# Routing of a two-block kernel spread over its steps, weights by tanh, and an expert part without loops on two engines

## What is computed

```python
mu, cov = mean and grouped covariance of x over all tokens        # groups of 16 channels
wm  = five Newton steps for the inverse root of cov
x   = gamma0 * (wm @ (x - mu)) + beta0
t   = layernorm(x)
a   = softmax(t . t[window of 33 tokens] / 8) @ t[window]         # same tokens are queries, keys, values
y   = x + layernorm(a) * gamma1 + beta1
n   = layernorm(y)
probs  = softmax(n @ router.T)                                    # 8 experts
rw, re = top_k(probs, 2);  rw = rw / sum(rw)
out = y + n + sum over the chosen e of rw[e] * (gelu(n @ w1[e] + b1[e]) @ w2[e] + b2[e])
```

## Time and profile before

| | |
|---|---|
| median of three timed runs | 1159.38 us |
| lowest and highest | 1153.58 and 1163.94 us |
| the profiled execution | 1151.54 us, its span 1149.7 us |
| mean granted TensorE clock in it | 0.942 of full |
| instructions | 27099 |
| busy: PE, DVE, ACT, POOL | 1070.4, 912.9, 570.3, 148.5 us |
| second part, first L968 to the end of step 55 | 78.6 to about 539 us |
| expert part | about 578 to 1149 us |

### The profile page before, as it was taken

One profiled execution on the slowest core, in us unless ns is written; L12 is line 12 of the kernel. 1 busy time (PEld: TensorE's weight loads), 2 busy tenths in 40 slices (PEclk: granted clock), 3 DMA queues, 4 the chain that ended last, 5 costly groups with the idle time before them and its releaser, 6 DMA issues.

```text
span 1149.7 us, 27099 instructions
## 1 busy us (share of the span) xinstructions
PE 1070.4 (93%) x9158; PEld 707.9 (62%) x9158; DVE 912.9 (79%) x2575; ACT 570.3 (50%) x919; POOL 148.5 (13%) x179
## 2 busy tenths in 40 slices
PE   7957999999999999998699999999999999999998
PEld 7835777777777777777554555555555555555553
DVE  6943578968898989898888787777787877778785
ACT  0013455545555555554355555555555555555553
POOL 7021222212222222222100000000000000000000
PEclk9956699959999999998599999999999999999999
DMA  9504355544545555555112222222222222222221
GB/s 291 219 8 92 87 140 129 129 101 117 139 121 141 128 131 136 129 135 121 54 49 64 71 68 68 70 66 72 65 71 68 68 72 64 71 71 65 71 68 45
DMA packets 244738, 111.41 MB, mean 97 GB/s; under 512 B 199392, under 2 KB 242656, under 8 KB 243888
## 3 DMA queue, kind: packets, MB, share of 16 engines
q1 hardware_dynamic: 235456, 96.91, 33.7%
q10 hardware_dynamic: 8064, 12.85, 3.3%
q0 software_dynamic: 1136, 0.56, 0.2%
HBM read 71.60 MB, written 38.67 MB: 96 GB/s over the span
## 4 chain that ended last, share of the span: by engine, by line
PE 69%; DVE 17%; ACT 6%; issue 3%; DMA 2%; SPq 1%; POOL 0%; DVEq 0%; ACTq 0%; POOLq 0%
PE p L1127 16%; PE p L1102 15%; PE p L1112 9%; PE p L1076 5%; PE p L960 5%; PE p L1049 4%; PE p L953 3%; PE p L970 3%; ACT prob L558 3%; DVE arena L646 2%; DVE t_s L816 2%; PE p L1071 2%; ACT xt_s L506 2%; DMA resid<-in_x_dram 2%; PE p L1123 2%
## 5 line engine op out<-in xcount | busy, mean ns | idle before, releaser
L575 ACT ACTIVATE arena<-p,b_s 128x896 f32<-128x896 f32 x224 | 225.4, 1007 | 245.9 <-PE p L1102 245.2
L869 DVE TENSOR_TENSOR arena<-arena,p 128x896 f32<-128x896 f32 x224 | 242.8, 1084 | 91.7 <-PE p L1112 88.3
L1127 PE MATMUL p<-arena,w_s 128*64 128x448 f32 x896 | 215.3, 559 | 0.3 <-DVE arena L869 0.3
L1102 PE MATMUL p<-thl,w_hi 128*128 128x448 f32 x448 | 164.8, 449 | 0.5 <-DVE thl L843 0.5
L1102 PE MATMUL p<-thl,w_lo 128*128 128x448 f32 x448 | 127.6, 366 | 0.0
L1112 PE MATMUL p<-arena,selector 128*128 128x448 bf16 x448 | 123.8, 358 | 3.6 <-DVE arena L869 3.2
L1112 PEld LDWEIGHTS p<-arena,selector 128*128 128x128 bf16 x448 | 25.4, 97 | 160.9 <-issue 115.6
L1102 PEld LDWEIGHTS p<-thl,w_hi 128*128 128x128 f32 x448 | 85.6, 192 | 21.1 <-issue 0.6
L464 POOL TENSOR_TENSOR yb<-yb,bet 128x448 f32<-128x448 f32 x56 | 59.3, 1059 | 275.3 <-DVE xn_s L810 275.3
L1076 PEld LDWEIGHTS p<-arena 64*96 64x96 f32 x1568 | 78.4, 175 | 21.6 <-issue 21.6
L766 DVE TENSOR_REDUCE sm<-sq 128x14 f32<-128x896 f32 (+1 forms) x59 | 61.2, 1037 | 38.3 <-ACT sq L530 32.5
(11 more groups left out here) (176 smaller groups left out, 1675.8 us busy)
## 6 DMA issues: line engine op xcount, KB each, us to landing
tn_spill<-tnt_s ACTq DMA_DIRECT2D x56, 224.0 KB, 2.4
arena<-tn_spill SPq DMA_DIRECT2D x56, 224.0 KB, 3.3
t_s<-tn_spill SPq DMA_DIRECT2D x56, 224.0 KB, 2.5
arena<-in_x_dram SPq DMA_DIRECT2D x112, 96.0 KB, 2.3
xn_rows<-xn_s SPq DMA_DIRECT2D x56, 192.0 KB, 2.1
out_dram<-arena SPq DMA_DIRECT2D x112, 96.0 KB, 1.8
resid<-in_x_dram SPq DMA_DIRECT2D x6, 1568.0 KB, 15.4
v_a<-xn_rows SPq DMA_DIRECT2D x56, 168.0 KB, 3.3
```

The costliest lines, as they stand in the source:

```text
L575: a.activation(hid[:, j % 2, :].rearrange("p (h n) -> p h n", h=H), (p34 if j % 2 == 0 else p56)[:, :, 0:CH], ACT.Gelu, bias=b1_s[:, j:j + ...
L869: v.tensor_tensor(gated[:, j % 2, :].rearrange("p (h n) -> p h n", h=H), hid[:, j % 2, :].rearrange("p (h n) -> p h n", h=H), p01[:, :, 0: ...
L1102: last = t.matmul(bank[:, h, 0:CH], w[:, 128 * j:128 * (j + 1)], thl[:, c, h, :], start=(k == 0), stop=(k == 1))
L1127: last = t.matmul(p2[64 * h:64 * h + 64, 0:CH], w2_s[:, j, :], gated[:, j % 2, h * CH:(h + 1) * CH], start=False, stop=(j == 3))
```

## The change

- SyncE: the token loads of group g+3 are issued ahead of the rows of group g instead of behind them.
- Routing: 19 operations a pair (the copy is k = -1), one a step from step 13 on, in the slot ahead of the wait for the reciprocal root; in the seven drain steps two a step, the second in the slot behind t_s; then two a group in the expert part, behind gate 0 and gate 2, until all eight pairs are done in group 47. By the end of the drain three pairs are routed.
- The tile `logits` is gone. ScalarE copies the logits straight into `comb`, where the weights of the same tokens will be written later; k = -1 copies them from there.
- Weights: the first two pairs keep the exponential. From the third on ScalarE computes h = tanh(gap / 2), and the weights are 0.5 - 0.5 h and 0.5 + 0.5 h, three instructions without a reciprocal.
- Expert part: VectorE and ScalarE are written out group by group; TensorE and SyncE keep their loops.
- Before the first group of each pair VectorE waits for that pair's weights.

```diff
-        logits = sb("logits", [128, NB * CPI, E])
+ROUTE_STEPS = 19
+ROUTE_FROM = 13
...
+        def route_turn(g, slot):
+            if g < G:
+                return g - ROUTE_FROM if slot == 0 else -1
+            if g < G + 7:
+                return G - ROUTE_FROM + 2 * (g - G) + slot
+            return G - ROUTE_FROM + 14 + 2 * (g - G - 7) + slot
+        def route_at(g, slot):
+            n = route_turn(g, slot)
+            return (n // ROUTE_STEPS, n % ROUTE_STEPS - 1) if 0 <= n < NP * ROUTE_STEPS else (NP, None)
+        LATE = 2
...
             for g in range(G + 1):
+                if g + 3 < G:
+                    tokens_in2(g + 3)
                 if g < G:
                     rows_out(g)
-                if g + 3 < G:
-                    tokens_in2(g + 3)
                 if g > 0:
                     values_in(g - 1)
...
-                    a.activation(logits[:, cq * NB:(cq + 1) * NB, :], p2[:, CH:CH + NB * E].rearrange("p (b e) -> p b e", b=NB),
+                    to = comb[:, q * NB * EM:(q + 1) * NB * EM].rearrange("p (b e) -> p b e", e=EM)[:, :, 0:E]
+                    a.activation(to, p2[:, CH:CH + NB * E].rearrange("p (b e) -> p b e", b=NB),
                                  ACT.Copy).then_inc(s_ls, 1)
...
+            def share(g, slot):
+                im, k = route_at(g, slot)
+                if k == 11:
+                    assert im >= LATE
+                    wait(act, s_gap, im + 1)
+                    a.activation(top[:, 3, :], top[:, 2, :], ACT.Tanh, scale=0.5).then_inc(s_gexp, 1)
...
             def step3(g, c, has, i, first=0):
                 if has(0):
                     for j in range(first, 2):
                         gelu(g, c, j)
+                    share(G + 7 + g, 0)
...
                     gelu(g, c, 2)
                     gelu(g, c, 3)
+                    share(G + 7 + g, 1)
...
-            step3(1, 1, lambda d: d <= 1, 0)
-            step3(2, 0, lambda d: True, 1)
-            act.wait_ge(s_gap, NP)
-            a.activation(top[:, 3, :], top[:, 2, :], ACT.Exp).then_inc(s_gexp, 1)
-            step3(3, 1, lambda d: True, 1)
-            with act.Fori(2, G // 2 - 1) as i:
-                step3(i * 2, 0, lambda d: True, i)
-                step3(i * 2 + 1, 1, lambda d: True, i)
...
+            for g in range(1, G + 1):
+                step3(g, g % 2, lambda d, g=g: d <= g < G + d, g // 2)
...
+                if k < 0:
+                    dve.wait_ge(s_ls, CPI * (im + 1))
+                    v.tensor_copy(pick[:, 2], weights_of(im)).then_inc(s_top, 1)
+                    return
...
+                if k == 12 and im >= LATE:
+                    ins = v.tensor_scalar(top[:, 0, :], top[:, 3, :], 0.5, None, ALU.mult)
+                if k == 13 and im >= LATE:
+                    ins = v.tensor_scalar(top[:, 1, :], top[:, 0, :], -1.0, 0.5, ALU.mult, ALU.add)
+                if k == 14 and im >= LATE:
+                    ins = v.tensor_scalar(top[:, 2, :], top[:, 0, :], 0.5, None, ALU.add)
...
-                routed = None if im is None or c == 5 else 3 * ((c + 1) % 7)
-                if routed is not None:
-                    route(im, routed)
-                    route(im, routed + 1)
+                im, k = route_at(g, 0)
+                if im < NP:
+                    route(im, k)
...
-                if routed is not None:
-                    route(im, routed + 2)
+                im, k = route_at(g, 1)
+                if im < NP:
+                    route(im, k)
...
                         gate(g, c, j)
-                        for k in routing[j]:
-                            route(NP - 1, k)
+                        if j % 2 == 0:
+                            im, k = route_at(G + 7 + g, j // 2)
+                            if im < NP:
+                                route(im, k)
```

More of the change, by code:

```diff
@@ L281, in norms, with weights_of @@
             return lo, hi
-        def route_image(g, c):
-            im = g // 7 - (1 if c == 6 else 2)
-            return im if 0 <= im < NP - 1 and c != 5 else None
+        def weights_of(im):
+            span = NB * CPI * EM
+            return comb[:, im * span:(im + 1) * span].rearrange("p (t e) -> p t e", e=EM)[:, :, 0:E]
+        def route_turn(g, slot):
[8 more added lines that the diff above has]
+        LATE = 2
         blk = ctx.enter_context(nc.Block())
@@ L548, in step @@
                     act.dma_start(spill[q], tnt_s[:, sl, :]).then_inc(s_sp[sl], 16)
-                im = route_image(g, c)
-                if c == ROUTE_GEXP and im is not None:
+                im, k = route_at(g - 1, 0)
+                if k == 11 and im < LATE:
                     wait(act, s_gap, im + 1)
@@ L611, in _ @@
                     double(0, 0)
+                    share(G + 3, 1)
+                    assert route_at(G + 3, 1) == (LATE, 11)
                 if c == 5:
@@ L738, in route @@
                     return
-                if k == 12:
+                if k == 12 and im < LATE:
                     ins = v.tensor_scalar(top[:, 0, :], top[:, 3, :], 1.0, None, ALU.add)
-                if k == 13:
+                if k == 13 and im < LATE:
                     ins = v.reciprocal(top[:, 1, :], top[:, 0, :])
-                if k == 14:
+                if k == 14 and im < LATE:
                     ins = v.tensor_tensor(top[:, 2, :], top[:, 3, :], top[:, 1, :], ALU.mult)
+                if k == 12 and im >= LATE:
[4 more added lines that the diff above has]
+                    ins = v.tensor_scalar(top[:, 2, :], top[:, 0, :], 0.5, None, ALU.add)
                 if k == 15:
@@ L749, in route @@
                 if k == 17:
[L750 removed]
+                    v.tensor_tensor(weights_of(im),
                                     pick[:, 0], pick[:, 1], ALU.add).then_inc(s_comb, 1)
@@ L851, in parts_step @@
                     wait(dve, s_ct, g - 1)
+                    if g % CPI == 0:
+                        dve.wait_ge(s_comb, g // CPI + 1)
                     v.tensor_scalar(parts[:, 0], src, 1.0, None, ALU.mult).then_inc(s_cs, 1)
@@ L871, in gate, with step3 @@
                                 p01[:, :, 0:CH], ALU.mult).then_inc(s_gm, 1)
-            def step3(g, c, has, more=True, routing=((), (), (), ())):
+            def step3(g, c, has, more=True):
                 if has(0):
@@ L928, in _ @@
                     low(0, 0)
-            dve.wait_ge(s_comb, NP - 1)
             dve.wait_ge(s_t2, G)
-            for g in range(4):
-                routing = [(4 * g + j,) for j in range(4)] if g < 3 else [(12, 13), (14, 15), (16,), (17,)]
-                step3(g, g % 2, lambda d, g=g: d <= g, routing=routing)
-            dve.wait_ge(s_comb, NP)
-            with dve.Fori(2, G // 2 - 1) as i:
-                cur["fin"] = i - 1
-                step3(i * 2, 0, lambda d: True)
-                cur["fin"] = i
-                step3(i * 2 + 1, 1, lambda d: True)
-            step3(G - 2, 0, lambda d: True)
-            step3(G - 1, 1, lambda d: True, more=False)
-            step3(G, 0, lambda d: d > 0, more=False)
+            for g in range(G + 1):
+                step3(g, g % 2, lambda d, g=g: d <= g < G + d, more=g + 1 < G)
         @blk.tensor
```

12 lines of the change are left out of this document (removed).

## The result

| | before | after |
|---|---|---|
| median of four timed runs on one chip | 1156.48 us (1143.00 to 1163.94) | 1114.91 us (1111.22 to 1121.16) |
| ratio, 95% interval | | 0.968 (0.958 to 0.979) |
| the profiled execution | 1151.54 us, span 1149.7 | 1112.64 us, span 1110.9 |
| mean granted TensorE clock in it | 0.942 | 0.960 |

The changed kernel is 3.2% faster, where 3.5% was forecast; the profiled time of 1112.6 us stands beside a sum of 1117.1. The total hides that three terms came out differently. A ratio leaves out executions more than 1.5% above the fastest of their kernel, so it is not always the quotient of the two medians beside it.

The account below looks back on a forecast made before the run. TensorE's stream bounds the expert part; steady steps are held by late values or by VectorE's routing. 1151.5 - 19.9 - 12.1 - 2.4 = 1117.1, plus 2.0 to the timed runs: 1119 us, range 1106 to 1140.

Parts of the forecast that it names:

- Two waits, each holding the step alone: Steady steps: late values or VectorE's third routing operation each hold 7.9 us; removing one alone leaves the other.
- SP's order: SyncE queue, steady steps: tokens ahead of rows start the values 1.15 us earlier, so TensorE's waits for them go.
- The step's own size: Steady steps: 7.48 us instead of 7.92, over 45 steps 19.9 us less.
- rival 2: Steady steps: SyncE's cycle bites in part, steps of 7.65, 8 us more, 1127 us; chance 0.10.
- Routing in the steps: Steady steps: one routing operation in an idle slot; L826 returns to 2.51 us, the tn-transpose wait goes.
- The half-clock stretch: Steady steps, 236 to 262 us: if the 1.02 us values wait tipped the clock, the stretch goes, 12.1 us less.
- The expert part: Expert groups: 2.4 us less if Tanh needs no table load; 95 routing operations in 48 groups taken as costing 0.
- 3: Expert part: each Tanh loads tables twice, five at 2.4 us, 1131 us; chance 0.06.
- 4: Expert part: the operation behind gate 0 reaches TensorE whole, 22 us, 1141 us; chance 0.05.
- 5: Steady steps stay at 7.9 us and the half clock stays; only 2.4 us won, 1157 us; chance 0.07.
- 6: Steady steps: SyncE's serial queue becomes the bound, kernel slower, 1211 us if its cycle is 9.4; chance 0.04.
- Rival 1: TensorE's half clock stays or comes elsewhere while the rest holds, 12 us more, 1131 us; chance 0.18.

Follow-up runs that it names:

- e0_after: The changed kernel run once more, unaltered, on another group's chip: median 1111.8 us, ratio 0.964 to the kernel before.
- the experiments on the start: First three iterations: old queue order in changed kernel, ratio 0.973; new order in kernel before, 1146.8 us against 1152.3. Idle products before step 1 in changed kernel: 0.970.

## Why the prediction was right, and where it was not

- **Two waits, each holding the step alone.** Right for what holds: only the kernel with both edits has most of its steps at 7.42 (27 and 32; 2 before, 10 and 11 with one half). Wrong as "taking away one alone would leave the other": the queue alone wins two thirds of the time, and 0.21 of the 0.36 us of pace. The reading took one step with a 0.56 us third operation for all of them, and did not count that three of seven steps have less there.
- **SP's order.** Right: values start 4.2 us into the step on average where it was 5.2, and at best 3.5 where it was 4.7. The step's own size was the failed term: 7.57 (7.56 in e0_after) instead of 7.48, 4 us over the 46. It comes from late values, as in rival 2, but not from one cause. Of 19 late values of the changed kernel that were issued in a steady step at full clock, 5 stood behind rows whose issue took over 2 us instead of 1.14 (five more such rows did no harm), 7 behind rows for whose landing SyncE waited 2.4 us or more instead of 1.25 (one more did no harm), and 7 were issued 3.5 to 4.1 us into the step and landed late all the same. The sum allowed 0.06 us a step for late values, and they cost 0.15; its landing of 1.25 us was read at one moment at the end of the part, where no token loads are left.
- **Routing in the steps.** Right: no L971 wait in any kernel with the spread routing; L845 at 2.51.
- **The half-clock stretch.** The cause was right and the size was not. It was a chance of falling that shrank, not a stretch that went. With the old order the three profiled executions fell five times in the steady steps, with the new order and nothing held back or moved seven of them fell six times. One fall was left in the profiled execution (two steps, 6.2 us, where the one before had cost 12.1), none in e0_after. 32.0 were forecast for steps 8 to 55 and 21.4 measured; of the 10.6 between them 46 x (7.573 - 7.48) = 4.3 are the pace and 21.31 - 2 x 7.48 = 6.3 this fall. In e0_after, where nothing fell, it is 391.03 - 362.76 = 28.3.
- **The start.** Not in the sum at all, and the largest miss: 13.3 us. The half clock of 0.58 from 94 to 139 us stood in the same profile, with a 2.05 us wait at its head that is shorter with the reordered queue (the experiments on the start leave open how much of the 13.3 us that is); I had looked only at the steady steps. It filled the hole that the two terms above left, so the total was near partly by luck.
- **The expert part.** Right in size (2.4 here, and 2.9 in the nine other profiled executions with the Tanh: 549.14 us instead of 552.04) and in that 95 operations in 48 groups cost nothing. Two routing operations and two final additions (L927) of it:

```profile
559.63 0.56 DVE L746 TENSOR_TENSOR arena<-arena,rank 128x392 f32<-128x392 f32 x1
...
564.37 0.56 DVE L748 TENSOR_REDUCE top<-arena 128x49 f32<-128x392 f32 x1
565.23 0.62 DVE L927 TENSOR_TENSOR arena<-p,t_s 128x448 f32<-128x448 f32 x1
...
575.26 0.61 DVE L927 TENSOR_TENSOR arena<-p,t_s 128x448 f32<-128x448 f32 x1
```

  The period is 575.26 - 565.23 = 10.03 us, as in the groups without routing. Only the reason needs care: Exp in ScalarE's idle time costs 0.76, so the 2.4 us in the earlier trace rows can't be the loads alone. Whether the Exp's place, ahead of the first Gelu of its group, or the four routing operations beside it made the rest wasn't tried.
- **Rivals.** 3 and 4 (tables beside Tanh, the operation behind gate 0) and 5 and 6 did not happen. Rival 1 happened in the profiled execution at half its price, rival 2 at about half of its 0.17 us a step.

## What to carry to other kernels

When two waits hold a step, sort the steps by the start of the waiting instruction within its step and not by the waits that the profile lists: that shows how many steps each one holds, and what removing one alone gives. A wait of half a microsecond on TensorE in front of a dense stretch costs more than itself, because some of them are followed by a stretch at half clock that costs 5 to 15 us; order a DMA queue so that what TensorE needs next doesn't stand behind what it needs three steps later. And look at every stretch in which the clock is low, the start of the kernel included, and ask which wait stands at its head.

## What the runs showed of the hardware

- TensorE's clock falls from 2.4 to 1.2 GHz behind waits as short as 0.37 us in a stream that is otherwise dense, but not every time: 0 of 461 steady steps with a wait for the values under 0.3 us, 11 of 95 from 0.3 to 0.75, 11 of 26 above.
- A Tanh between Gelus loads no table: two loads in the whole kernel (1.28 us each), none beside the six Tanhs. An Exp in the same places brings two loads each.
- SyncE's issue of the same two row transfers took 1.14 us as a rule and over 2 in 10 of 46 steady steps of the changed kernel. Over nine kernels with the new order it was not the issue closest behind the token loads that took long: of 243 that began within 0.5 us of them 6 took over 2 us, of 64 that began 1.0 to 1.5 us behind them 34. Why, no run separates.
